# A gated state-space block with a 1.58-bit feed-forward part on one core: the feed-forward steps in another order, and the setup in halves

## The chip, the cores and the metric

The kernel runs on one core of a Trainium2 chip. The metric is the device time of one execution in microseconds (us), lower is better. The kernel before takes 265.46 us (median of 3 runs, 264.85 to 266.59).

## What is computed

`x` is [4 batches, 256 tokens, 256 channels], the context [4, 256, 128]. Cut to what matters:

```python
xc    = causal depthwise conv (4 taps) of in_proj_w @ ctx        # [256, 256] per batch
u     = silu(xc + conv_b)
x_dbl = x_proj_w @ u                 # 40 rows: 8 for delta, 16 B, 16 C
delta = softplus(dt_proj_w @ x_dbl[:8] + dt_proj_b)
state = state * exp(delta * A) + (delta * u) * B   # over 256 tokens, 16 states per channel
y     = (sum over states of state * C + D * u) * silu(layernorm(x))
x     = x + tanh(g_xattn) * y
h     = act_quant(layernorm(x))                    # 8 bit, per token
inter = silu(h @ w_gate.T) * (h @ w_up.T)          # [256, 1024] per batch, ternary weights
x     = x + tanh(g_ffn) * act_quant(hadamard(inter)) @ w_down.T
```

## The kernel before

Everything is written out by hand per engine; each engine runs its list in order, and semaphores tie the lists together. There is no scheduler.

*The scan.* The 16 states of a batch are taken two at a time: 8 steps per batch, 32 in all. Step g needs on ScalarE four exponentials (`decays`, line 823), on GpSimd the input term token by token (`drives`, line 1105), on TensorE its transposes into PSUM (`drive_rows`, 407) and the row of C spread over the partitions (`C_rows`, 447), on VectorE two scans (`scan`, 1230) and one product (`times_C`, 1272), and on TensorE the sum (`accumulate`, 463). In the loops over `k` (batch) and `s` (step, g = 8k + s) VectorE runs `scan(g + 1)` and then `times_C(g)`. The transposes of step g wait for the scan that last read their bank.

*The feed-forward part.* While batch k is scanned, batch f = k - 1 is normalised, quantised to 8 bits and sent through gate and up, and batch p = k - 2 gets its Hadamard transform, quantisation and down product, each in pieces for the two halves of 128 tokens, t = 0 and 1. In order: `residual`, `stats2` (VectorE, 1292 to 1302), `rstd2` (ScalarE, 907), `second_rstd` (1311), `second_norm` (ScalarE), `token_scale` (1326), `scale_tokens` (ScalarE, 923), `round_tokens` (1341), `tokens_T` (TensorE, 557), `gate` (593), `silu_gate` (ScalarE, 929), `up` (593), `gate_times_up` (VectorE, 1352), three folds on GpSimd (`fold_tile`, 1130), `inter_T` (612), `inter_out` (ScalarE, 933), `hadamard_mm` (632), `absmax2` (VectorE, 1360), `quant_down` (ScalarE, 939), `round_down` (1368), `q2_T` (649), `q2_out`, `down` (659), `result` (1380). After the last batch the same pieces run without a scan beside them: the tail.

*The front of a batch.* `in_proj` (492) multiplies the context by four weight copies, one per tap; `silu_u` gives u; `x_dbl` (508) gives rows for B and C and 8 rows for delta, which `dt_rows` copies and `dt_proj` (525) multiplies; `softplus` (889 to 894, ScalarE) with `softplus_tail` (GpSimd) gives delta; `high_pieces` and `split` (1283 to 1285) cut B and C into three bf16 parts; `du_T` turns delta * u. For batch 0 the projection runs without taps (`first_in_proj`, 370), ScalarE and VectorE add the taps (`first_conv`, 1242), and VectorE does the tail of softplus itself (`delta_on_vector`, 1250 to 1254). The PSUM bank X holds the transposes, projections and delta rows of batches 2 and 3 in turn, which is where many waits come from.

*The setup.* SyncE issues the loads in one order: first context, in_proj_w, conv_b, x_proj_w, dt_proj_w, dt_proj_b, D, the other contexts, w_gate, x, w_up, w_down. VectorE takes the three sums |w| (`weight_abs`, 1385), the first before, the second behind the statistics of x (`first_norm`, 1409), the third in step 0.

```python
def silu_gate(f, t):
    act.wait_ge(pe_gate, LC * f + t + 1)
    act.wait_ge(dve_gs, f + 1)
```

## Time and profile before

| | |
|---|---|
| median of 3 runs | 265.46 us (264.85 to 266.59) |
| profiled execution, its own time | 265.58 us |
| its span, first to last instruction | 263.8 us |
| mean granted TensorE clock | 0.883 of full |
| busy: TensorE / VectorE / ScalarE / GpSimd | 187.3 / 213.9 / 157.3 / 147.5 us |
| start of `residual` of batches 0, 1, 2, 3 | 82.65 / 127.54 / 174.37 / 219.89 us |

The span is 1.8 us shorter than the time of the same execution; what lies around it is the same for both kernels. A time in the rows below is counted from the first instruction. The four starts of `residual` cut the span into setup with batch 0, batches 1, 2 and 3, and tail.

### The profile page before, as it was taken

The page shows a single profiled execution, that of the slowest core. Times are in us where ns is not written, and L with a number is a line of the kernel's source. Part 1 is how long each engine was busy: PE and PEld are TensorE (multiplying, and loading weights), DVE is VectorE, ACT ScalarE, POOL GpSimd, SP SyncE. Part 2 cuts the span into 40 slices and gives each one's busy share as a digit, 9 for nine tenths or more (in the row PEclk, how much of TensorE's full clock was granted, in tenths as well). Part 3 has the DMA queues.
Part 4 walks back from the last instruction along what each step waited for, and adds up shares of the span by engine and source line. Part 5 has one row for each costly group of instructions (what it writes and reads, how often), then busy time and mean ns, then how long its engine had stood idle before and what let it go on. Part 6 is the DMA issues. An engine that isn't in the chain of part 4 may idle for free. (4 is left out here: it accounts for less than half of the span.)

```text
span 263.8 us, 3694 instructions
## 1 busy us (share of the span) xinstructions
PE 187.3 (71%) x1209; PEld 155.8 (59%) x1216; DVE 213.9 (81%) x340; ACT 157.3 (60%) x271; POOL 147.5 (56%) x213
## 2 busy tenths in 40 slices
PE   3779489895595569867667787675596768474945
PEld 2547388794494468647557666564485547342944
DVE  4489997898989499579989897998959775579872
ACT  1685996949234556994776799735748504650040
POOL 1100890999961096039999942999930399008500
PEclk9999855899779559999997999999979988989597
DMA  3891000000000000000000000000000000000001
GB/s 60 268 363 75 1 4 0 0 1 2 0 0 2 0 0 1 2 1 0 0 2 0 0 20 4 20 4 0 0 0 24 0 20 2 0 0 1 20 22 40
DMA packets 8149, 6.34 MB, mean 24 GB/s; under 512 B 2202, under 2 KB 7874, under 8 KB 8130
## 3 DMA queue, kind: packets, MB, share of 16 engines
q1 hardware_dynamic: 7154, 6.02, 7.1%
q10 hardware_dynamic: 976, 0.09, 0.3%
q8 instruction: 10, 0.16, 0.3%
q14 instruction: 9, 0.07, 0.1%
HBM read 5.05 MB, written 1.05 MB: 23 GB/s over the span
## 5 line engine op out<-in xcount | busy, mean ns | idle before, releaser
L1105 POOL TENSOR_SCALAR driveT<-duT,BT 128x256 f32<-128x256 f32 x120 | 62.2, 538 | 41.0 <-issue 21.3
L823 ACT ACTIVATE decay<-delta,zero_c,aneg 128x255 f32<-128x255 f32 x128 | 65.2, 589 | 1.7 <-DVE delta L1254 1.6
L1230 DVE TENSOR_TENSOR_SCAN state<-decay,BC 128x512 f32<-128x512 f32 x30 | 36.4, 1213 | 4.4 <-issue 4.3
L1272 DVE TENSOR_TENSOR prod<-state,BC 128x1024 f32<-128x1024 f32 x32 | 38.5, 1204 | 0.6 <-issue 0.6
L463 PE MATMUL PY<-id,prod 128*128 128x128 f32 x256 | 37.9, 297 | 1.4 <-DVE x L1294 1.0
L1230 DVE TENSOR_TENSOR_SCAN state<-decay,UP 128x512 f32<-128x512 f32 x30 | 35.8, 1193 | 0.0
L463 PEld LDWEIGHTS PY<-id,prod 128*128 128x128 f32 x256 | 32.8, 154 | 2.5 <-issue 1.2
L447 PE MATMUL BC<-bc,sel 96*128 96x256 bf16 x64 | 13.1, 288 | 27.4 <-DVE prod L1272 27.3
L1130 POOL TENSOR_TENSOR wnat<-wnat 128x512 f32<-128x512 f32 x18 | 22.9, 1274 | 15.9 <-DVE wnat L1352 15.2
L933 ACT COPY hT<-GP 128x1024 f32<-128x1024 f32 x8 | 8.1, 1010 | 35.0 <-PE GP L612 35.0
L407 PE MATMUL BC<-id,driveT 128*128 128x128 f32 x120 | 21.2, 305 | 10.9 <-POOL driveT L1105 10.8
L407 PEld LDWEIGHTS BC<-id,driveT 128*128 128x128 f32 x120 | 16.0, 161 | 14.6 <-POOL driveT L1105 12.8
L447 PEld LDWEIGHTS BC<-bc,sel 96*128 96x128 bf16 x64 | 5.2, 101 | 32.7 <-issue 31.6
L1131 POOL TENSOR_TENSOR wnat<-wnat 128x512 f32<-128x512 f32 x18 | 22.9, 1275 | 0.0
L407 PE MATMUL UP<-id,driveT 128*128 128x128 f32 x120 | 20.0, 293 | 0.8 <-DVE state L1230 0.8
L407 PEld LDWEIGHTS UP<-id,driveT 128*128 128x128 f32 x120 | 15.6, 153 | 1.5 <-issue 1.5
L593 PE MATMUL GP<-wT,qT 128*128 128x512 bf16 x49 | 13.0, 381 | 3.5 <-ACT wq L929 2.7
L1352 DVE SCALAR_TENSOR_TENSOR wnat<-GP,us,wq 128x1024 f32<-128x1024 f32 x7 | 9.0, 1284 | 7.2 <-issue 5.6
L612 PE MATMUL GP<-id,wnat 128*128 128x128 f32 x64 | 9.9, 306 | 5.1 <-POOL wnat L301 3.2
L300 POOL TENSOR_TENSOR wnat<-wnat 128x160 f32<-128x160 f32 x6 | 4.1, 684 | 14.9 <-DVE wnat L1352 14.6
L280 POOL TENSOR_SCALAR spa<-spe 128x512 f32<-128x512 f32 x3 | 1.9, 619 | 18.4 <-ACT spl L894 18.4
L612 PEld LDWEIGHTS GP<-id,wnat 128*128 128x128 f32 x64 | 8.4, 160 | 5.8 <-DVE wnat L301 3.5
(208 smaller groups left out, 412.7 us busy)
## 6 DMA issues: line engine op xcount, KB each, us to landing
wnat<-in_L_ffn_w_gate_dram SPq DMA_DIRECT2D x1, 1024.0 KB, 9.6
xs<-in_x_dram SPq DMA_DIRECT2D x1, 1024.0 KB, 12.0
wnat<-in_L_ffn_w_up_dram SPq DMA_DIRECT2D x1, 1024.0 KB, 11.5
wnat<-in_L_ffn_w_down_dram SPq DMA_DIRECT2D x1, 1024.0 KB, 11.3
out_dram<-ot SPq DMA_DIRECT2D x8, 128.0 KB, 1.7
ctxs<-in_ctx_dram SPq DMA_DIRECT2D x1, 384.0 KB, 7.1
ctxs<-in_ctx_dram SPq DMA_DIRECT2D x1, 128.0 KB, 2.8
inw<-n_L_xattn_in_proj_w_dram SPq DMA_DIRECT2D x1, 128.0 KB, 2.6
```

The costliest lines, as they stand in the source:

```text
L407: last = nc.tensor.transpose(drive_bank(h)[:, L * n + P * c:L * n + P * (c + 1)], driveT[:, m % RING, c, n, P * h:P * (h + 1)], id32[:])
L447: last = nc.tensor.matmul(PC[:, L * n:L * (n + 1)], row_pick(DS + NB * j + n), bc3[:, b, :], start=True, stop=True)
L463: last = nc.tensor.matmul(PY[:, E * c + P * h:E * c + P * (h + 1)], prod[:, g % RING, h, n, P * c:P * (c + 1)], id32[:], is_transpose=True ...
L593: last = nc.tensor.matmul(ffn_bank(f, t)[:, 512 * i:512 * (i + 1)], qT[:, h, P * t:P * (t + 1)], w[:, h, 512 * i:512 * (i + 1)], start=(h ...
L612: last = nc.tensor.transpose(GP[:, P * a:P * (a + 1)], fold[:, t, P * a:P * (a + 1)], id32[:])
L823: last = nc.scalar.activation(decay[:, m % RING, h, n, 1:L], delta[:, b % 2, h, 1:L], ACT.Exp, bias=zero_c[:], scale=aneg[:, h, NB * j + n ...
L1105: last = nc.gpsimd.tensor_scalar(driveT[:, m % RING, c, n], duT[:, b % 2, c], BT[:, b % 2, c, NB * j + n:NB * j + n + 1], 1.0, ALU.mult, A ...
L1130: nc.gpsimd.tensor_tensor(dst[:, :, 0, :], src[:, :, 0, :], src[:, :, 1, :], ALU.add)
L1131: nc.gpsimd.tensor_tensor(dst[:, :, 1, :], src[:, :, 0, :], src[:, :, 1, :], ALU.subtract).then_inc(done, 1)
L1230: nc.vector.tensor_tensor_scan(state[:, g % STATES, h].rearrange("p n l -> p (n l)"), decay[:, g % RING, h].rearrange("p n l -> p (n l)"), ...
L1272: nc.vector.tensor_tensor(prod[:, g % RING].rearrange("p h n l -> p h (n l)"), state[:, g % STATES].rearrange("p h n l -> p h (n l)"), PC. ...
L1352: nc.vector.scalar_tensor_tensor(out=inter[:, t], in0=ffn_bank(f, t)[:], scalar=us[:, t:t + 1], in1=sg[:, t], op0=ALU.mult, op1=ALU.mult). ...
```

## The change

*Setup.* delta comes from u by one product: `delta_weights` multiplies x_proj_w's first 8 rows by dt_proj_w once (into `dtuT`, 256 x 256), and `delta_raw(n)` is four calls of u by that matrix instead of `dt_rows` and `dt_proj`'s two calls on 8 rows; `x_dbl` has 96 columns instead of 104. The first projection, the first convolution, the first u, the first driving terms and the exponentials signal by halves of the 256 channels. On TensorE the transposes of dt_proj_w, which wait for x_proj_w too, stand ahead of `first_in_proj`. x is loaded ahead of the other contexts and w_gate, dt_proj_w on ScalarE's queue. `first_norm` stands ahead of the first delta and ahead of all three sums |w|, which follow behind the first drives, in step 0 and in step 1. The copies `inwT` and `ctxT` on ScalarE stand behind the first delta and behind decays(0) and decays(1); `in_proj(1)` needs both.

*Steps.* The diff of the loops, cut to the places spoken of (`up(f, 0)` follows `gate(f, 0)`; `hadamard_mm(f, 0)` and `absmax2(p, 0)` are earlier; GpSimd runs five steps ahead):

```diff
+LEAD = 5
             def up(f, t):
-                if f == B - 1:
-                    pe.wait_ge(act_sg, LC * f + t + 1)
-                elif t == 0:
-                    pe.wait_ge(act_sg, LC * f + 2)
-                else:
-                    pe.wait_ge(dve_mul, LC * f + 1)
+                pe.wait_ge(act_sg, LC * f + t + 1)
...
             setup()
+            delta_weights_T()
             first_in_proj()
-            setup_weights()
+            delta_weights()
+            setup_rows()
...
                     if s == 3:
-                        if k == 0:
-                            du_T(1)
+                        if k < B - 1:
+                            du_T(k + 1)
+                        if new:
+                            gate(f, 0)
                         if old:
                             down(p, 0)
-                        if new:
-                            gate(f, 0)
-                        if front:
+                        if k == 0:
                             in_proj(n, 1)
+                        if new:
+                            up(f, 0)
                     if s == 4:
...
+                        if new:
+                            gate(f, 1)
+                            up(f, 1)
...
                     if s == 7:
...
-                            inter_T(f, 0)
+                            hadamard_mm(f, 0)
...
                     if s == 0:
+                        if old:
+                            quant_down(p, 0)
+                        if new:
+                            rstd2(f)
                         if 1 <= k < B - 1:
                             softplus(k + 1)
...
             p, f = B - 2, B - 1
+            absmax2(p, 0)
             residual(f)
```

The first place on TensorE's list, from its start: before,

```order
L343 MATMUL GP<-id,ctxs 128x128 x2
L347 MATMUL GP<-id,inw 128x128 x2
L370 MATMUL GP<-ctxT,xn 128x256 x2
L354 MATMUL PY<-id,xpw 128x40 x2
L358 MATMUL BC<-id,dtw 104x128 x2
L363 MATMUL UP<-id,inwk 128x128 x8
L508 MATMUL GP<-u,xpwT 104x256 x2
L525 MATMUL GP<-dtlo,dtwT 128x256 x2
```

and now (dtw are dt_proj_w's rows, xn holds in_proj_w turned, dtuT the product of the two small weights):

```order
L355 MATMUL GP<-id,ctxs 128x128 x2
L359 MATMUL GP<-id,inw 128x128 x2
L373 MATMUL BC<-id,dtw 8x128 x2
L366 MATMUL GP<-ctxT,xn 128x256
L366 MATMUL X<-ctxT,xn 128x256
L380 MATMUL BC<-dtwT,xpw 128x256
L380 MATMUL UP<-dtwT,xpw 128x256
L386 MATMUL PY<-id,xpw 128x40 x2
L550 MATMUL GP<-u,dtuT 128x256 x2
L550 MATMUL UP<-u,dtuT 128x256 x2
L532 MATMUL GP<-u,xpwT 96x256 x2
```

The dt_proj_w transposes moved ahead of the first projection, the tap copies (L363) went behind the delta product, and delta no longer waits for `x_dbl`.

The second place is VectorE at the turn from batch 1 to batch 2. Before:

```order
L1272 TENSOR_TENSOR prod<-state,BC 128x1024
L1230 SCALAR_TENSOR_TENSOR state<-decay,BC 128x512
L1230 SCALAR_TENSOR_TENSOR state<-decay,UP 128x512
L1272 TENSOR_TENSOR prod<-state,BC 128x1024
L1292 TENSOR_TENSOR PY<-PY,szT 128x512
L1294 TENSOR_TENSOR x<-PY,xs 128x512
```

and now:

```order
L1272 TENSOR_TENSOR prod<-state,BC 128x1024
L1228 SCALAR_TENSOR_TENSOR state<-decay,BC 128x512
L1228 SCALAR_TENSOR_TENSOR state<-decay,UP 128x512
L1360 TENSOR_REDUCE am<-GP 128x1
L1361 TENSOR_SCALAR am<-am 128x1
L1362 RECIPROCAL sc<-am 128x1
L1363 TENSOR_SCALAR dq<-am,wdn 128x1
L1272 TENSOR_TENSOR prod<-state,BC 128x1024
L1292 TENSOR_TENSOR PY<-PY,szT 128x512
L1294 TENSOR_TENSOR x<-PY,xs 128x512
```

`absmax2(p, 0)` now stands behind the second next scan, one step earlier, between the batches' products; it needs the Hadamard product of step 7.

The third place is TensorE at steps 3 and 4 of batch 2 (qT the quantised tokens, q the same before the transpose, driveT the driving terms). Now:

```order
L459 MATMUL X<-id,du 128x128 x4
L616 MATMUL GP<-wT,qT 128x512 x4
L679 MATMUL UP<-wT,q2T 128x256 x8
L616 MATMUL GP<-wT,qT 128x512 x4
L432 MATMUL BC<-id,driveT 128x128 x4
L432 MATMUL UP<-id,driveT 128x128 x4
L472 MATMUL BC<-bc,sel 128x256 x2
L488 MATMUL PY<-id,prod 128x128 x8
L669 MATMUL UP<-id,wq 128x128 x8
L616 MATMUL GP<-wT,qT 128x512 x8
```

The second L616 is `up(f, 0)`, so driveT's transposes and everything behind stand behind the first silu; the last one is `gate(f, 1)` and `up(f, 1)` together. Before, both gates came first, with one step's pieces between them, and each `up` a step later.

## Rows read from the trace of the kernel before

**Rows 1.** The page: busy time of each engine, its share of the span.
```profile
PE 187.3 (71%) x1209; PEld 155.8 (59%) x1216; DVE 213.9 (81%) x340; ACT 157.3 (60%) x271; POOL 147.5 (56%) x213
```

**Rows 2.** Stretches: us, busy us of PE, PEld, DVE, ACT, POOL, PEclk, DMA, GB/s.
```profile
33.07:45.11 12.04, 11.46 (x44) 9.69 (x45) 10.66 (x11) 9.66 (x21) 6.68 (x11) 0.50 0.01 2
45.11:82.65 37.54, 29.04 (x220) 26.27 (x218) 33.79 (x34) 24.00 (x46) 30.80 (x43) 0.86 0.00 1
82.65:127.54 44.89, 32.31 (x203) 26.48 (x205) 36.36 (x53) 29.41 (x55) 22.43 (x31) 0.85 0.00 1
127.54:174.37 46.83, 34.34 (x263) 29.14 (x266) 42.87 (x66) 34.79 (x58) 37.93 (x53) 0.96 0.02 7
174.37:216.54 42.17, 28.74 (x220) 24.01 (x222) 35.88 (x57) 23.11 (x34) 26.79 (x37) 0.95 0.02 7
216.54:219.89 3.35, 3.31 (x18) 3.31 (x19) 0.00 (x1) 0.00 (x0) 3.27 (x3) 0.59 0.02 5
```

**Rows 3.** Timeline, setup, TensorE: start, us, line, tiles [idle before].
```profile
5.32 2.08 PE L370 MATMUL GP<-ctxT,xn 128*128 128x256 f32 x4 [0.52 <-DVE xn L1428]
8.76 0.43 PE L354 MATMUL PY<-id,xpw 40*128 40x40 f32 x2 [1.37 <-DMA dtw<-n_L_xattn_dt_proj_w_dram]
14.36 2.07 PE L525 MATMUL GP<-dtlo,dtwT 8*128 8x256 f32 x4 [0.45 <-ACT dtlo L879]
22.27 3.76 PE L492 MATMUL GP<-ctxT,inwT 128*128 128x256 f32 x8 [0.52 <-ACT ctxT L991]
```

**Rows 4.** Timeline, setup, ScalarE and VectorE.
```profile
7.57 1.02 ACT L965 ACTIVATE conv<-GP,cb,cw 128x256 f32<-128x256 f32 x2 [3.04 <-PE GP L370]
11.08 0.72 ACT L978 ACTIVATE u<-conv,zero_c 128x512 f32<-128x512 f32 x1 [0.57 <-DVE conv L1242]
...
14.29 2.29 DVE L1385 TENSOR_REDUCE wsum<-wnat 128x1 f32<-128x2048 f32 x1 [3.25 <-DMA wnat<-in_L_ffn_w_gate_dram]
23.50 0.69 DVE L1254 TENSOR_TENSOR delta<-spl,spr 128x512 f32<-128x512 f32 x1
39.05 0.40 DVE L1283 TENSOR_TENSOR bc<-GP,high 64x256 bf16<-64x256 f32 x1
```

**Rows 5.** Timeline, batch 0, VectorE: two roundings of the weights.
```profile
57.24 1.26 DVE L1397 TENSOR_SCALAR wq<-wnat 128x2048 bf16<-128x2048 f32 x1
62.73 3.00 DVE L1397 TENSOR_SCALAR wq<-wnat 128x2048 bf16<-128x2048 f32 x1 [0.89 <-POOL wnat L1136]
```

**Rows 6.** Timeline, start of batch 1, VectorE.
```profile
86.34 1.22 DVE L1230 TENSOR_TENSOR_SCAN state<-decay,BC 128x512 f32<-128x512 f32 x1
...
92.19 0.34 DVE L1311 TENSOR_SCALAR ve<-mv,r 128x1 f32<-128x1 f32 x2 [3.52 <-ACT r L908]
```

**Rows 7.** Timeline, batch 2, steps 2 to 5, TensorE, ScalarE, VectorE.
```profile
146.69 2.00 PE L632 MATMUL GP<-had,hT 128*128 128x128 f32 x16
155.31 1.21 ACT L929 ACTIVATE wq<-GP,zero_c,gs 128x1024 f32<-128x1024 f32 x1
157.72 1.21 ACT L929 ACTIVATE wq<-GP,zero_c,gs 128x1024 f32<-128x1024 f32 x1 [0.60 <-PE GP L593]
159.05 1.03 PE L593 MATMUL GP<-wT,qT 128*128 128x512 bf16 x4
160.17 1.28 DVE L1352 SCALAR_TENSOR_TENSOR wnat<-GP,us,wq 128x1024 f32<-128x1024 f32 x1 [1.30 <-issue]
```

**Rows 8.** Timeline, end of batch 3 and tail, TensorE and VectorE.
```profile
216.58 1.97 PE L463 MATMUL PY<-id,prod 128*128 128x128 f32 x8 [0.40 <-DVE prod L1272]
218.34 1.51 PE L472 MATMUL PY<-diag,u 128*128 128x128 f32 x8
...
228.96 3.30 PE L632 MATMUL BC<-had,hT 128*128 128x128 f32 x16
232.74 0.91 PE L593 MATMUL GP<-wT,qT 128*128 128x512 bf16 x3 [0.49 <-DVE qT L1345]
...
228.39 1.22 DVE L1360 TENSOR_REDUCE am<-UP 128x1 f32<-128x1024 f32 x1
```

More of the change, by code:

```diff
@@ L31 @@
 DVE_COLS = 88
-DT0 = 96
+ROWS = 3 * 2 * DS
 class Chain:
@@ L171, in gated_ssm_ffn @@
         bank6, bank7 = UP[:, 0:512], UP[:, 512:1024]
-        mean1, ve1, nt1 = (UP[:, 8 * i:8 * (i + 1)] for i in range(3))
+        first = sb("first", [P, 3, B * LC])
+        mean1, ve1, nt1 = (first[:, i] for i in range(3))
         wgT = wT[:, 0].rearrange("p (h i) -> p h i", h=HALF)
@@ L348, in setup, with first_in_proj, delta_weights_T, delta_weights @@
                 last.then_inc(pe_setup, 1)
-            def setup_weights():
-                pe.wait_ge(ld_small, 16 * 2)
+            def first_in_proj():
+                pe.wait_ge(dve_setup, 2)
+                for h in range(HALF):
+                    nc.tensor.matmul(first_half(h), inw0T[:, P * h:P * (h + 1)], ctxT[:, 0, :],
+                                     start=True, stop=True).then_inc(pe_xin0, 1)
+            def delta_weights_T():
+                pe.wait_ge(ld_small, 16 * 2)
+                for h in range(HALF):
+                    last = nc.tensor.transpose(PC[0:DR, P * h:P * (h + 1)], dtw[:, h], id32[:])
+                last.then_inc(pe_setup, 1)
+            def delta_weights():
+                pe.wait_ge(act_dtw, 1)
+                for h in range(HALF):
+                    nc.tensor.matmul(delta_weight_bank(h), xpw[0:DR, P * h:P * (h + 1)], dtwT[:],
+                                     start=True, stop=True).then_inc(pe_setup, 1)
+            def setup_rows():
                 for h in range(HALF):
@@ L356, in setup_weights, with setup_taps @@
                 last.then_inc(pe_setup, 1)
-                for h in range(HALF):
-                    last = nc.tensor.transpose(PB[0:DT0 + DR, P * h:P * (h + 1)], dtw[:, h], id32[:])
-                last.then_inc(pe_setup, 1)
-                pe.wait_ge(dve_inwk, 2)
-                for k in range(DC):
+            def setup_taps(part):
+                pe.wait_ge(dve_inwk, part + 1)
+                pe.wait_ge(act_spread, 1)
+                for k in range(2 * part, 2 * part + 2):
                     for h in range(HALF):
@@ L364, in setup_weights @@
                 last.then_inc(pe_setup, 1)
-            def first_in_proj():
-                pe.wait_ge(dve_setup, 2)
-                for h in range(HALF):
-                    last = nc.tensor.matmul(bank4[:, L * h:L * (h + 1)], inw0T[:, P * h:P * (h + 1)], ctxT[:, 0, :],
-                                            start=True, stop=True)
-                last.then_inc(pe_xin, 1)
             def setup_late():
                 pe.wait_ge(ld_ctx, 16)
-                pe.wait_ge(act_setup, 1)
+                pe.wait_ge(dve_xpw, 1)
                 for b in range(1, B):
@@ L1018, in _ @@
                             softplus(1)
-                            gate_out(0)
-                        if new:
-                            rstd2(f)
-                        if old:
-                            quant_down(p, 0)
                         if new:
@@ L1081, in _ @@
             second_norm(f)
+            inter_out(p, 1)
             scale_tokens(f)
-            inter_out(p, 1)
-            quant_down(p, 0)
             silu_gate(f, 0)
@@ L1152, in _ @@
             last.then_inc(pool_diag, 1)
-            drives(DVE_DRIVES)
+            for m in range(DVE_DRIVES, LEAD):
+                drives(m)
             norm_z(0)
-            for m in range(DVE_DRIVES + 1, AHEAD):
-                drives(m)
             for k in range(B):
```

376 lines of the change are left out of this document (181 added, 195 removed).

## Prediction, made before the changed kernel was run

> **What bounds the kernel now.** I read the page first: no engine is full; VectorE is the busiest with 213.9 of 263.8 us [rows 1]. Then the stretches between the four starts of `residual` [rows 2]. VectorE's idle time is a stretch's length less its busy time: batch 1 44.89 - 36.36 = 8.5 us, batch 2 46.83 - 42.87 = 4.0 us, batch 3 up to its last product 42.17 - 35.88 = 6.3 us, then 3.35 us with VectorE empty, until TensorE has summed the last state. The scan is a chain through VectorE (no step can begin before its list reaches it), so a microsecond saved there is saved in the span, and one hidden elsewhere is not. Then the timeline at the largest waits: in the setup VectorE waits 3.25 us for w_gate [rows 4]; in batch 1 it waits 3.52 us for the second norm's root, which on ScalarE stands behind a whole softplus [rows 6]; gate times up waits in each batch, 1.30 us in batch 2 [rows 7]. The change touches all three places, so the question is what stands there afterwards. VectorE's work is the same but for one small copy taken over from ScalarE.
>
> The sum is a walk through the new lists with the durations of the rows, stretch by stretch, against the profiled execution (span 263.8, time 265.58, so 1.8 us around it); its time is 0.12 us above the median of the runs, which I neglect.
>
> **Setup and batch 0: -0.6 us.** `first_in_proj` runs at 5.32 now [rows 3]. In the new list the transposes of dt_proj_w stand ahead of it, and they wait for two loads, x_proj_w's too. Today both have landed at 8.76, where TensorE's wait ends [rows 3]; ScalarE's first tap starts at 7.57 [rows 4]. The landing of the two with dt_proj_w on the other queue isn't shown: it lies between 5.32 (no delay) and 8.76 (as today). I take 7.7, nearer to the late end, since x_proj_w stays behind conv_b in its queue. Then 0.7 us of transposes, 1.0 us for half a product (2.08 for two), and the first tap starts at 9.5 instead of 7.57. The halves give back a little, and u(0) ends at 13.5 instead of 11.80 (+1.7). `delta_raw` doubles the calls: `dt_proj` takes 2.07 for two, so four take 4.1, but ScalarE starts on the first half after 2.05. In place of `x_dbl`, a copy and `dt_proj` that makes 17.7 for the end of delta's product. After softplus and VectorE's tail, delta starts its last operation at 22.4 instead of 23.50: -1.1, because the statistics of x (3.4 us) now fill the wait in which VectorE stood for the weights.
>
> That gain is spent at once. The first sum |w| (2.29 us) was in that wait and is now in line. And `in_proj(1)` needs `ctxT`, whose copy stands behind decays(1): TensorE idles from about 27 to 31.3 and then needs 3.76 for the first half of the projection, as at 22.27 [rows 3], and about 1.9 for the second. It ends at 37.3, u(1), `x_dbl(1)` and the cast of its rows follow, and VectorE's `split(1)`, at 39.05 today [rows 4], starts at 40.7 after a wait of 3.3 us. Scan 3 starts at 47.5 instead of 45.11: +2.4. From there to `residual(0)` the same work follows. VectorE's idle time there is 37.54 - 33.79 = 3.8 us, of which some 2 go (the weights' sum is long ready, drives are five ahead), and a rounding that took 3.00 against 1.26 for the same tile [rows 5] falls behind GpSimd's scaling: -1. Together -0.6; bounds -2.5 (loads at 5.32) and +2.5 (loads at 8.76, nothing of the idle time gained).
>
> On that rounding: the 3.00 us one starts with GpSimd scaling the next weights. The Trainium skill says (SBUF — State Buffer, section "SBUF: two separate sides") that VectorE and GpSimd share one pair of SBUF ports, held for a whole instruction by whoever started first. By that rule slow roundings come back wherever they meet a GpSimd pass, and the last 1 us would not be gained; the sum would be 1 us higher. On the loads it says (DMA: Bandwidth & Descriptors, section "Issuing engines are not separate DMA queues") that the queues of two engines run on the same DMA engines and that a second queue saves only issue time. By that rule the two loads land at 8.76 as before, and the setup costs 1.0 us more; no row here shows these loads on different queues.
>
> **Batch 1: +0.9 us.** The 8.5 us of waits go. `rstd2` stands ahead of softplus, so the 3.52 us vanish. What is late next: `second_norm` still stands behind softplus(2), which waits for `delta_raw(2)`. TensorE's clock is low there, and two calls of `dt_proj` took 2.07 at the low clock [rows 3], so four take about 4: x's norm comes 1.1 us after VectorE is ready for it. The scaled tokens come 1.0 late. `up(0, 0)` stands right behind `gate(0, 0)` and waits for the silu, which on ScalarE stands behind the tokens' copy, an exponential group, a copy of duT and a table load; VectorE waits 3.2 us for the first gate times up and 0.6 for the second. Sum of new waits 5.9. Then the early `absmax2(0, 0)` falls into this stretch: 1.7 us of work (an absmax of this form is 1.22, [rows 8], its three small ones the rest) and a wait: after the last product of batch 1 TensorE needs the rows of C, the sum (0.9 at full clock), D * u (0.9) and the Hadamard product (2.00, [rows 7]), 4.05 together, against 2.25 for two scans (1.22 each, overlapping a little, [rows 6]): 1.8. 44.9 - 8.5 + 5.9 + 3.5 = 45.8.
>
> **Batch 2: +2.5 us.** 4.0 of idle go. One absmax goes out and one comes in, with 1.8 of wait. The tokens and the Hadamard of half 1 are 0.7 late. `quant_down(0, 1)` ends 1.5 after VectorE wants to round it: it stands behind the tokens' copy, which waits for TensorE's transposes behind the scan. Gate times up: today both gates' silus (155.31 and 157.72) come before `up` at 159.05 and VectorE waits 1.30 [rows 7]. Now `up(1, 0)` follows the first silu at once, about 2.5 us sooner, but VectorE wants it 2.25 + 1.1 sooner, and copy_duT is ahead: 1.8. The second gate now waits for the first gate times up, then comes its silu behind a copy of q2, then `up`: 6.0 us from `up` to `up` against 4.6 of work: 1.1 (the rest overlaps). New waits 6.9, less 0.4 of slow small operations: 46.8 - 4.0 + 6.9 - 0.4 = 49.3.
>
> **Batch 3 to its last product: -4.2 us.** 6.3 of idle go, absmax2(1, 0) is already done (1.7), the new waits are 1.5 + 1.2 + 1.1 + 0.6 and some small ones, 4.6, less 0.8 of slow roundings: 42.2 - 6.3 - 1.7 + 4.6 - 0.8 = 38.0.
>
> **Tail: +2.2 us.** VectorE stands empty for 3.35 us [rows 2] while TensorE does the last sum (1.97) and D * u (1.51) [rows 8]. The new list has `inter_T` ahead of that sum and the Hadamard product behind it, and `absmax2(2, 0)` stands ahead of `residual(3)`. At TensorE's full clock that is 0.9 + 0.9 + 0.9 + 2.0 and absmax2 1.7, 5.9 us until `residual(3)`; at half clock, as the 0.59 of that stretch says of today [rows 2], up to 8.3. I take 6.8: +3.4. In return absmax2 (228.39) and its rounding leave the chain between the tokens and their transpose. But today the Hadamard of half 1 (3.30) covers them, and the gate at 232.74 starts right behind it [rows 8]. Now that product is ahead of the tokens' transpose and bound by `inter_out` on ScalarE: gain 1.2. Bounds 0 and +4.4.
>
> Sum: -0.6 + 0.9 + 2.5 - 4.2 + 2.2 = +0.8, so 265.58 + 0.8 = 266.4; I say 266.5.
>
> **Rivals.** (1) The walk counts every handover in full, and the new waits are half of what it says: TensorE keeps the full clock through batches and tail and the two loads land early. Then tail 0 instead of +2.2, setup -2.5 instead of -0.6: 266.4 - 2.2 - 1.9 = 262.3. For it: the clock is 0.96 and 0.95 in batches 2 and 3 [rows 2], and `inter_T` fills a gap. Against it: 0.59 at the end, and first_in_proj's wait is in the list. (2) Slower: the Hadamard product at each turn runs at the low clock. It took 3.30 and not 2.00 in the tail [rows 7, 8]; the turn then costs 1.3 more in batches 1 and 2, and the tail takes its bound (+2.2): 266.4 + 4.8 = 271.2. It decides from about 0.85 granted at the turns. The Trainium skill (TensorE: Matmul & The Clock Gate, section "What's actually happening") says that the throttled clock is the default and activity releases it; the trace agrees, 0.50 after TensorE's pause before 33.07 [rows 2]. By that rule the longer pauses before each `up` speak for this rival. (3) The change doesn't do what it says: x lands no earlier, first_norm runs behind 17 us as today, and the first delta comes 2 us later: 268.4.
>
> **How the numbers follow.** My forecast 0.45, rival 1 0.25, rival 2 0.23, rival 3 0.07. About 1% is what a measurement of this kernel can tell from no change: 262.8 and 268.1 are the bounds. Of my forecast's 0.45 (264.0 to 269.0) 0.38 lie within, 0.02 below and 0.05 above; rival 1 gives 0.21 faster, 0.04 same; rival 2 is all slower; rival 3 half slower. Faster 0.23, same 0.45, slower 0.32. The range reaches to both rivals: 261.0 to 271.5.
>
> **What would show it.** Right: the gap ahead of L1311 is gone in batch 1; VectorE waits some 1.8 us ahead of absmax2 at both turns and 4 or more in the tail; the first tap starts after 9 us; split(1) waits about 3 us. Wrong: absmax2 without a wait, the first tap before 8 us, or batch 2 shorter than 46.8 us.

## The result and the profile after

The changed kernel takes 273.42 us (median of 4 runs, 272.92 to 276.38) where the kernel before, run beside it on the same chip, takes 266.02: a ratio of 1.029, 95% interval 1.020 to 1.039. It is slower by 7.4 us. The prediction was 266.5 us with a range up to 271.5. It had the sign right (+0.8 us) and missed the size: a time within 1% of the kernel before was held likeliest, and the measured one lies outside the range.

The profiled execution of after is its longest, 276.38 us with a span of 274.6; the other three have spans of 271.1 to 271.8. Executions of one kernel differ here, so the places come from the profiles and the sizes from the medians. Ratios and their intervals leave out executions more than 1.5% above a kernel's fastest and medians don't, so the two can differ, most for abs0_behind_stats, whose ratio rests on two of its twelve executions.

The page of after, busy time by engine, against [rows 1]:

```profile
PE 190.8 (70%) x1232; PEld 157.9 (58%) x1236; DVE 215.2 (78%) x341; ACT 155.5 (57%) x268; POOL 146.9 (53%) x212
```

VectorE has 1.3 us more work in a span 10.8 us longer: this is waiting. The stretches, cut as in [rows 2] (the first from scan 3, the next from `residual` to `residual`; columns as there):

```profile
45.83:83.98 38.15, 28.05 (x206) 24.55 (x206) 34.86 (x35) 22.13 (x42) 29.30 (x41) 0.87 0.00 1
83.98:129.26 45.28, 34.21 (x239) 28.42 (x240) 38.50 (x58) 33.00 (x60) 32.58 (x43) 0.96 0.01 1
129.26:180.51 51.25, 37.22 (x267) 31.41 (x268) 42.12 (x66) 34.64 (x59) 38.58 (x55) 0.90 0.02 6
180.51:222.84 42.33, 29.91 (x191) 25.00 (x193) 33.47 (x53) 18.69 (x29) 17.90 (x24) 0.79 0.02 7
222.84:230.18 7.34, 5.66 (x40) 5.47 (x38) 1.58 (x6) 1.01 (x1) 4.03 (x4) 0.82 0.00 0
```

Length less VectorE's busy time is its idle time: 9.1 us in batch 2 and 8.9 in batch 3, against 4.0 and 6.3 before. All the waits of VectorE over a microsecond between `residual(1)` and `residual(3)` (timeline; the bracket holds the idle time ahead and what ended it, `issue` where the profile shows nothing that did):

```profile
145.61 0.45 DVE L1341 TENSOR_SCALAR q<-xn 128x512 bf16<-128x512 f32 x1 [1.69 <-ACT xn L940]
153.49 0.70 DVE L1368 TENSOR_SCALAR wq<-ctxs 128x1024 bf16<-128x1024 f32 x1 [2.26 <-ACT ctxs L956]
159.58 1.28 DVE L1352 SCALAR_TENSOR_TENSOR wnat<-GP,us,wq 128x1024 f32<-128x1024 f32 x1 [1.65 <-issue]
165.24 1.28 DVE L1352 SCALAR_TENSOR_TENSOR wnat<-GP,us,wq 128x1024 f32<-128x1024 f32 x1 [1.03 <-issue]
177.74 1.22 DVE L1360 TENSOR_REDUCE am<-GP 128x1 f32<-128x1024 f32 x1 [1.88 <-PE GP L652]
195.44 0.43 DVE L1341 TENSOR_SCALAR q<-xn 128x512 bf16<-128x512 f32 x1 [1.92 <-ACT xn L940]
197.36 1.23 DVE L1360 TENSOR_REDUCE am<-GP 128x1 f32<-128x1024 f32 x1 [1.49 <-PE GP L652]
204.69 0.69 DVE L1368 TENSOR_SCALAR wq<-ctxs 128x1024 bf16<-128x1024 f32 x1 [2.27 <-ACT ctxs L956]
210.32 1.28 DVE L1352 SCALAR_TENSOR_TENSOR wnat<-GP,us,wq 128x1024 f32<-128x1024 f32 x1 [1.19 <-issue]
215.98 1.28 DVE L1352 SCALAR_TENSOR_TENSOR wnat<-GP,us,wq 128x1024 f32<-128x1024 f32 x1 [1.03 <-issue]
228.54 1.22 DVE L1360 TENSOR_REDUCE am<-GP 128x1 f32<-128x1024 f32 x1 [5.69 <-PE GP L652]
```

The new waits have names: the rounding of half 1 (L1368, twice), the absmax at the turn (177.74; the turn of batch 1 has the same 1.88 at 126.49) and in the tail (228.54), and q (L1341). The four gate-times-up operations (L1352) each start 1.1 us after TensorE has begun the `up` that they need, at 158.45, 164.11, 209.19 and 214.85. In the tail, the first gate product starts 20.1 us after the last product (242.92), and 16.2 us in before (232.74 in [rows 8] less 216.54 in [rows 2]).

The setup (timeline; ScalarE's rows, then VectorE's, against [rows 3, 4]):

```profile
6.59 0.56 ACT L984 ACTIVATE conv<-GP,cb,cw 128x256 f32<-128x256 f32 x1 [0.98 <-PE GP L366]
10.79 0.29 ACT L987 ACTIVATE tg<-gates,zero_c 128x2 f32<-128x2 f32 x1 [2.99 <-DMA alog<-in_L_xattn_A_log_dram]
11.91 0.51 ACT L992 ACTIVATE u<-conv,zero_c 128x256 f32<-128x256 f32 x1
...
13.83 2.71 DVE L1409 BATCH_NORM_STATS2 st<-xs 128x6 f32<-128x256 f32 x8 [3.44 <-DMA xs<-in_x_dram]
17.94 0.43 DVE L1248 TENSOR_SCALAR spa<-spe 128x512 f32<-128x512 f32 x1 [0.44 <-ACT spe L908]
21.18 0.69 DVE L1254 TENSOR_TENSOR delta<-spl,spr 128x512 f32<-128x512 f32 x1
38.90 0.42 DVE L1283 TENSOR_TENSOR bc<-GP,high 64x256 bf16<-64x256 f32 x1 [1.09 <-ACT high L893]
```

delta comes 2.3 us earlier than before (21.18 against 23.50), but `split(1)` at 38.90 against 39.05 keeps 0.15 of that, and `residual(0)` starts 1.3 us late.

### The profile page after: what moved, and what is told of

It is laid out like the page before. It is cut to its first block and busy times, and to the rows that moved or that the text cites. A ratio compares the mean times of both kernels' runs of the same rounds, so it can differ in the third digit from the quotient of the medians.

```text
span 274.6 us, 3736 instructions
## 1 busy us (share of the span) xinstructions
PE 190.8 (70%) x1232; PEld 157.9 (58%) x1236; DVE 215.2 (78%) x341; ACT 155.5 (57%) x268; POOL 146.9 (53%) x212
## 5 line engine op out<-in xcount | busy, mean ns | idle before, releaser
L488 PE MATMUL PY<-id,prod 128*128 128x128 f32 x256 | 40.8, 312 | 2.9 <-DVE x L1294 2.9
L488 PEld LDWEIGHTS PY<-id,prod 128*128 128x128 f32 x256 | 35.7, 164 | 4.2 <-issue 3.6
L432 PE MATMUL BC<-id,driveT 128*128 128x128 f32 x120 | 19.2, 285 | 10.7 <-DVE state L1228 9.2
L432 PEld LDWEIGHTS BC<-id,driveT 128*128 128x128 f32 x120 | 14.8, 150 | 14.3 <-issue 10.8
L616 PE MATMUL GP<-wT,qT 128*128 128x512 bf16 x52 | 13.6, 380 | 13.1 <-ACT wq L946 10.6
L432 PEld LDWEIGHTS UP<-id,driveT 128*128 128x128 f32 x120 | 14.7, 150 | 5.6 <-issue 4.9
L1352 DVE SCALAR_TENSOR_TENSOR wnat<-GP,us,wq 128x1024 f32<-128x1024 f32 x7 | 9.0, 1284 | 10.6 <-issue 10.6
L616 PEld LDWEIGHTS GP<-wT,qT 128*128 128x128 bf16 x56 | 4.7, 98 | 19.5 <-ACT wq L946 13.6
L635 PE MATMUL GP<-id,wnat 128*128 128x128 f32 x64 | 10.9, 326 | 6.2 <-POOL wnat L315 3.2
L1360 DVE TENSOR_REDUCE am<-GP 128x1 f32<-128x1024 f32 x5 | 6.1, 1225 | 11.0 <-PE GP L652 10.9
```

Source lines behind the costliest of these rows:

```text
L432: last = nc.tensor.transpose(drive_bank(h)[:, L * n + P * c:L * n + P * (c + 1)], driveT[:, m % RING, c, n, P * h:P * (h + 1)], id32[:])
L488: last = nc.tensor.matmul(PY[:, E * c + P * h:E * c + P * (h + 1)], prod[:, g % RING, h, n, P * c:P * (c + 1)], id32[:], is_transpose=True ...
L616: last = nc.tensor.matmul(ffn_bank(f, t)[:, 512 * i:512 * (i + 1)], qT[:, h, P * t:P * (t + 1)], w[:, h, 512 * i:512 * (i + 1)], start=(h ...
L635: last = nc.tensor.transpose(GP[:, P * a:P * (a + 1)], fold[:, t, P * a:P * (a + 1)], id32[:])
```

## Experiments

Thirteen runs of twelve kernels, on several chips, each beside the kernel before on one chip. "Against before" is the difference of these two medians; the median of before itself lies between 265.23 and 266.65 us from chip to chip.

| kernel | median us | against before | ratio, 95% interval |
|---|---|---|---|
| after | 273.42 | +7.4 | 1.029 (1.020 to 1.039) |
| setup_alone | 268.62 | +3.4 | 1.010 (1.005 to 1.014) |
| abs1_back | 272.14 | +6.9 | 1.022 (1.015 to 1.029) |
| tail_only | 271.80 | +5.2 | 1.019 (1.014 to 1.024) |
| abs0_behind_stats | 267.87 | +2.6 | 0.994 (0.986 to 1.001) |
| all_three | 263.69 | -3.0 | no interval |
| all_three_again | 263.31 | -2.3 | 0.982 (0.974 to 0.990) |
| before_rstd_first | 264.05 | -1.2 | 0.994 (0.990 to 0.999) |
| setup_rstd_first | 267.48 | +0.8 | 1.004 (1.000 to 1.008) |
| delta_twice | 270.77 | +4.7 | 1.016 (1.010 to 1.023) |
| rows_in_loop | 263.23 | -2.4 | 0.990 (0.987 to 0.994) |
| norm_first | 264.05 | -2.0 | 0.992 (0.988 to 0.997) |
| norm_scale_first | 266.04 | 0.0 | 0.995 (0.990 to 1.000) |
| before_norm_first | 265.13 | -1.0 | 0.997 (0.993 to 1.002) |

**setup_alone: one part of the change alone.** The new setup, delta from u and scans by halves, with the four engines' loops in the order of before. Against before, in TensorE's loop:

```diff
                     if s == 0:
                         if k == 0:
-                            dt_proj(1)
+                            delta_raw(1)
                             gate_T(0)
                         if 1 <= k < B - 1:
-                            dt_proj(k + 1)
+                            delta_raw(k + 1)
```

> The changed setup, delta from u by one product, and the scans that start by halves, with the loops of the four engines in the order of the kernel before. Theory A (the new order of the feed-forward part makes the loss, by waits that it puts on VectorE): the setup and batch 0 cost 1.3 us more than before (83.98 against 82.65 us to the first residual), the rest is as before, so 267.3 us (265.5 to 269). Theory B (the setup leaves the whole program with a lower granted clock, 0.842 against 0.883, and the loss comes with it): 271 us or more, and batches 2 and 3 longer than before's 46.8 and 42.2 us even in the old order.

268.6 us, 3.4 over before: above theory A's value but in its range, below theory B's. Its batch 2 is 48.3 us long, 1.5 longer than before's, and its batch 3 is 40.6, 1.6 shorter, so B's two longer batches aren't there, nor is B's lower clock (0.890 in its profile, 0.883 in before's). The new setup with delta from u has a cost of its own, and by these medians a somewhat larger part of the loss, 4.0 us, is the order's. In batch 1 the wait that the full change removes is longer than in [rows 6]:

```profile
94.98 0.33 DVE L1332 TENSOR_SCALAR ve<-mv,r 128x1 f32<-128x1 f32 x2 [5.05 <-ACT r L936]
```

**abs1_back: one row of the order undone.**

```diff
                     if s == 3:
                         if new:
                             round_tokens(f)
-                        if old:
-                            absmax2(p, 1)
...
                         scan(g + 1, 0)
                         scan(g + 1, 1)
...
                     if s == 3:
                         if k == 0:
                             weight_means()
+                        if old:
+                            absmax2(p, 1)
```

> After, with the absolute maximum of the second half (absmax2(p, 1)) moved back behind the scans of slot 3. Theory A: ahead of the scans it holds them by 1.9 us with its wait and 1.7 with its work; TensorE's drive rows of that slot wait for the scans, the transposes of q stand behind the drive rows, ScalarE's copy of qT behind those, and its scaling for round_down(p, 1) behind that; so the waits of 2.26 and 2.27 us ahead of round_down(p, 1) and of 1.49 ahead of absmax2(1, 1) all go: 4 to 6 us off 273.4, 268.5 us (267 to 270.5). Theory B (TensorE at 1.2 GHz is what is late, whatever stands ahead): the wait ahead of round_down(p, 1) shrinks by less than half and others grow, 272.5 to 274.

The waits went as theory A says: none ahead of the rounding L1368 and of absmax2(1, 1) is left over 0.5 us in batches 2 and 3. This shows the chain of theory A, with one number put right: the 1.9 us is q's wait (195.44 above), and absmax2's own is 1.49 in batch 3 and nearly nothing in batch 2 (146.15, right behind q). Batches 2 and 3 are 50.1 and 40.6 us long, 1.1 and 1.7 shorter than after's. But batch 1, in which the edit changes nothing, took 48.1 us here and 45.3 in after, so stretches of one list differ by more than that between two executions. The median fell only by 1.3 us (0.5 against before), and the intervals of the two ratios overlap. It lies between the two theories' ranges, nearer to B's. Alone the edit is worth little; see all_three.

**abs0_behind_stats and tail_only: two microseconds of work put into a wait.**

```diff
-                        if old:
-                            absmax2(p, 0)
                     times_C(g)
                     if s == 0:
                         if new:
                             residual(f)
                             stats2(f, dve_ln_link.begin(dve, f))
+                        if old:
+                            absmax2(p, 0)
```

and the same in the tail, with `rstd2` ahead of `quant_down(p, 0)` on ScalarE in both places. tail_only has the edit in the tail alone.

> After, with absmax2(p, 0) behind residual and stats2 at both turns and in the tail, and ScalarE's rstd2 ahead of its quant_down(p, 0). Theory A: residual and stats2 (2.4 us at 129.26 to 131.7) cover the wait of 1.88 us at both turns and 2.6 of the 5.69 us in the tail: 6.4 us less, of which about 1.2 comes back where round_down(p, 0) of batch 3 has no split ahead of it; 268.2 us (266.5 to 270). Rival (the Hadamard product of the tail is the end of another chain, so that residual comes earlier but the first gate product doesn't): the turns' 3.8 us alone, 269.6, or with the turns' gain lost in q's wait too, 272 to 273.

> After, with absmax2(p, 0) behind residual and stats2 in the tail alone (and rstd2 ahead of quant_down(p, 0) there); the turns stay. In abs0_behind_stats the first gate product came 17.6 us after the last product, against 20.1 in after and 16.2 in before. If the tail's order is worth that alone, 2.5 us go: 270.9 us (269.5 to 272), and the other 3 of the 5.5 us that abs0_behind_stats gained are the turns' (1.88 us, twice). Rival: the tail holds all 5.5 us and the turns' waits come back elsewhere, 268 us.

267.9 us as theory A had it, and 271.8 for the tail alone, inside its range. By the medians against before, the tail's part is 2.2 us (7.4 to 5.2) and the turns' 2.6 (5.2 to 2.6), not the 3.8 of two waits: 1.2 us stand ahead of `round_down` in batch 3, as expected. That the two together are a gain is clear (ratios of 1.029 and 0.994, with intervals apart), but how it splits isn't: the ratios 1.029, 1.019 and 0.994 give the turns the larger part, while in the profiles the tail alone is 5.5 us shorter (46.24 us in tail_only, 46.16 in abs0_behind_stats, 51.76 in after, from the last product to the end). What is left in abs0_behind_stats:

```profile
151.85 0.69 DVE L1368 TENSOR_SCALAR wq<-ctxs 128x1024 bf16<-128x1024 f32 x1 [1.65 <-ACT ctxs L956]
165.26 1.28 DVE L1352 SCALAR_TENSOR_TENSOR wnat<-GP,us,wq 128x1024 f32<-128x1024 f32 x1 [2.69 <-issue]
182.17 2.00 DVE L1368 TENSOR_SCALAR wq<-ctxs 128x1024 bf16<-128x1024 f32 x1 [1.16 <-ACT ctxs L956]
225.09 0.70 DVE L1292 TENSOR_TENSOR PY<-PY,szT 128x512 f32<-128x512 f32 x1 [3.74 <-PE PY L497]
```

**all_three: both, and the tanh of the gates behind u(0).**

```diff
-            act.wait_ge(ld_gate, 16 * 3)
-            nc.scalar.activation(tg[:], gates[:], ACT.Tanh, bias=zero_c[:]).then_inc(act_gate, 1)
             for h in range(HALF):
                 ...
             last.then_inc(act_u, 1)
+            act.wait_ge(ld_gate, 16 * 3)
+            nc.scalar.activation(tg[:], gates[:], ACT.Tanh, bias=zero_c[:]).then_inc(act_gate, 1)
```

> After with absmax2(p, 0) behind stats2 (turns and tail), absmax2(p, 1) behind the scans, and the tanh of the gates with its wait for the last load behind u(0). By the runs so far: 267.9, less 1.3 to 2.8 for absmax2(p, 1) (its medians and the two batches of its profile), less at most 0.4 for the tanh, since VectorE is at the first norm, for which x lands at 13.8, until 17.5 and waited 0.44 us for softplus behind it, however early u(0) is: 265.5 us (263.5 to 267), level with before. Rival (each wait removed is taken up by the next in line, q's and the gate products'): 267 to 268.5, no gain over abs0_behind_stats. Second rival (the early u(0) starts the whole chain of the setup earlier): first residual at 81 us and not at 83, 263 us.

> The same kernel as all_three, beside rows_in_loop on one chip, for an interval against before: 263.7 us by the first call, so a ratio of 0.985 to 0.995 if that holds.

263.7 and 263.3 us: 10 us faster than after, under the expected 265.5, and faster than before, by 1.8% by the ratio of the second run (just past the expected 0.985) and 0.9% by its medians. In all_three's profile u(0) began its second half at 10.36 instead of after's 11.91, and delta came 0.55 us earlier relative to x's landing (20.26 with x at 13.45, against 20.79 with x at 13.43 in abs0_behind_stats). So the tanh was worth half a microsecond to delta; at `residual(0)` (82.84 and 81.85 in the two profiles, 82.27 in abs0_behind_stats) no gain can be told. The stretches of batches 1 to 3, in all_three_again and in abs0_behind_stats:

```profile
81.85:125.88 44.03, 34.55 (x227) 27.98 (x228) 36.93 (x53) 30.41 (x57) 29.54 (x40) 0.92 0.01 1
125.88:173.10 47.22, 36.27 (x271) 30.13 (x270) 42.07 (x66) 35.76 (x61) 37.55 (x53) 0.93 0.02 7
173.10:214.51 41.41, 28.23 (x206) 23.91 (x205) 34.93 (x57) 20.47 (x31) 22.16 (x29) 0.85 0.02 7
```

```profile
82.27:126.30 44.03, 34.30 (x226) 27.94 (x228) 36.94 (x53) 30.40 (x57) 29.54 (x40) 0.92 0.01 1
126.30:176.91 50.61, 36.21 (x270) 30.95 (x270) 42.22 (x65) 35.62 (x61) 39.64 (x56) 0.93 0.02 6
176.91:221.34 44.43, 27.76 (x205) 23.27 (x205) 36.06 (x57) 20.46 (x31) 19.65 (x27) 0.86 0.02 7
```

Batch 1 is the same to 0.01 us, at the same granted clock. Batches 2 and 3, the only ones in which absmax2(p, 1) stands, are 3.4 and 3.0 us shorter at nearly the same clock. So in this pair its place is worth 6.4 us, and in abs1_back's profile only 2.8. The direction agrees in the medians against before (4.9 to 5.6 us here with the tanh, 0.5 in abs1_back) and in the ratios (1.2% here, 0.7% there, with overlapping intervals), the size doesn't: batch 2 took 51.25 us in after and 53.84 in tail_only, whose lists are the same up to the tail. That the gains aren't additive is therefore likely but not shown. A reading that fits: in abs1_back the chain of absmax2(p, 0) at the turn still stood (its 1.88 us are in that profile at both turns); with that gone too, the chain of half 1 was the one that held both batches.

**before_rstd_first and before_norm_first: what of the change is good for the old kernel.** The first moves one call on ScalarE:

```diff
                     if s == 1:
...
-                        if new:
-                            rstd2(f)
...
                     if s == 0:
+                        if new:
+                            rstd2(f)
                         if 1 <= k < B - 1:
                             softplus(k + 1)
```

The second moves `softplus(k + 1)` behind `second_norm(f)` of slot 1 as well.

> The kernel before with one line moved on ScalarE: rstd2(f) ahead of softplus(k + 1) in slot 0. Theory A (the wait of 3.52 us ahead of L1311 in batch 1 is the one clear gain of the new order): 2.5 to 3.5 us faster than before, 263 us. Rival (the next wait, for scaled tokens or for the gate product, is late by the same chain and takes it): 265.5 to 266.5, and the waits behind it in batch 1 grow by what goes.

> before_rstd_first with second_norm(f) ahead of softplus(k + 1) too. Its norms weren't waited for (no wait ahead of amax in the loop), but the scaled tokens were, 1.33 and 1.23 us in batches 2 and 3, and the first gate product 2.54, 2.04 and 1.37. If the norm's place matters only where the longer product from u stands ahead of softplus: no gain, 264 us (263 to 265). If the chain norm, scale, q, gate starts earlier here too: 262 us.

The wait of 3.52 us of [rows 6] is gone and 1.2 us of the median with it, between theory and rival: part of it was taken up later, as in batch 2, where the first gate times up now waits 2.04 us (1.30 in [rows 7]). The norm's place adds nothing (1.0 us under before where the first had 1.2): softplus then stands between norm and scaling, and the wait is ahead of q (1.78 us in batch 1, where there was none).

**setup_rstd_first, delta_twice and rows_in_loop: the setup or the product from u?** The first is setup_alone with `rstd2` ahead of softplus. The second repeats the product:

```diff
                 for h in range(HALF):
-                    for i in range(HALF):
-                        last = nc.tensor.matmul(delta_half(n, h), dtuT[:, i, P * h:P * (h + 1)],
+                    for _ in range(2 if n > 0 else 1):
+                        for i in range(HALF):
+                            last = nc.tensor.matmul(delta_half(n, h), dtuT[:, i, P * h:P * (h + 1)],
                     ...
                     last.then_inc(pe_draw, 1)
```

The third takes it out of batches 1 to 3 of all_three, with rows of x_dbl copied by ScalarE and a second, shifted copy of dt_proj_w:

```diff
+                if n >= 1:
+                    pe.wait_ge(act_dtlo, n)
+                    for h in range(HALF):
+                        nc.tensor.matmul(delta_half(n, h), dtwT2[DT0:ROWS, P * h:P * (h + 1)], dtlo[DT0:ROWS, :],
+                                         start=True, stop=True).then_inc(pe_draw, 1)
+                    return
```

> setup_alone with rstd2 ahead of softplus. In setup_alone L1311's counterpart waited 5.05 us in batch 1, where before waited 3.52, since the eight products that make delta from u end later than the two of dt_proj did. Theory D (the product from u costs only by what stands behind softplus on ScalarE): the whole wait goes, and the time is that of before_rstd_first, 264.05, plus what the setup costs to the first residual, 0.9: 265 us (263.5 to 266.2). Theory E (the setup and the longer product cost by themselves, in TensorE's time and in the clock of what follows): the distance of 3.4 us between setup_alone and before stays, 267.4 us (266.3 to 269).

> setup_rstd_first with the eight products that make delta from u computed twice in slot 0 of batches 0 to 2 (the same operands into the same bank, the second product replaces the first; nothing else changes). One product group took 1.89 us on TensorE where the clock was granted at 2.4 GHz and 3.57 to 3.75 at 1.2. Theory F (the product from u is what setup_rstd_first pays over before_rstd_first, 3.4 us by their medians, 2 by their ratios to before, by way of softplus, the second norm and the waits for scaled tokens behind it): as much again per batch, 2 to 4 us over 267.5, so 270.5 us (269.5 to 272), with new waits of some 2 us ahead of amax in batches 1 and 2. Theory G (the product is covered; the setup itself holds the loss): 267.5 to 268.5.

> all_three with delta of batches 1 to 3 made as in the kernel before, from dt rows of x_dbl by two products of 8 rows (and ScalarE's dt_rows copy, 0.36 us, ahead of copy_BT); batch 0 keeps the product from u. delta_twice paid 3.3 us by the medians for computing the longer product once more in three batches. Theory F (the product from u costs 1 us or more a batch, in TensorE's time ahead of softplus): 263.7 less 2 to 3.5, 261 us (259.5 to 262.5), and below all_three_again of the same call. Theory G (with rstd2 ahead of softplus the product's place is covered, and what delta_twice paid was only the second one): level with all_three_again within 1 us.

By its time setup_rstd_first came out as theory E says. But the kernel before took 266.65 us on that chip and 265.23 on the one that the theories were worked out from, and against before, 0.8 us, it lies between the two (D -0.2, E 2.2). Of the 3.4 us, 2.6 went with the one call, but the same call gives before 1.2 us, so 2.0 stay between the two kernels. delta_twice spoke for the product as their cause (3.3 us for three repetitions, or 3.9 against before), though the waits came elsewhere than expected: ahead of amax there was 1.33 us in batch 1 (0.93 in setup_rstd_first) and none over 0.75 in batch 2, and ahead of absmax2(0, 0) 3.25 (1.52). rows_in_loop spoke against it: 263.2 us beside 263.3, as theory G says, and batches 1 to 3 of the two profiles, both with a granted clock of 0.864, agree to 0.4 us. (By the ratios, 0.990 and 0.982, it would even be the slower one.) In it the product in batch 1 was indeed short, and softplus began 5.6 us after `residual` instead of 7.6 in all_three. Part of what it gained there was lost on TensorE: its in_proj of batch 1 took 3.23 us, that of all_three 1.88, the duration at 2.4 GHz. TensorE's two products in rows_in_loop, then in all_three:

```profile
85.59 1.77 PE L557 MATMUL X<-dtlo,dtwT 8*128 8x256 f32 x4 [1.14 <-issue]
93.39 3.23 PE L522 MATMUL X<-ctxT,inwT 128*128 128x256 f32 x8
```

```profile
86.61 3.75 PE L550 MATMUL X<-u,dtuT 128*128 128x256 f32 x8 [0.27 <-issue]
93.01 1.88 PE L516 MATMUL X<-ctxT,inwT 128*128 128x256 f32 x8
```

So in the order of all_three the product from u costs nothing that can be measured. In the old order this wasn't tried: delta_twice shows that a second product costs there, not what the first one does. What makes the 2.0 us is therefore open. The setup can be a part of it: `residual(0)` starts at 83.1 us on the mean of the seven profiles that have the new setup with the tanh in its place, and at 82.2 on that of the three with the old setup. But the seven lie between 81.9 and 84.0, so even these 0.9 us aren't clear of the spread.

**norm_first and norm_scale_first: attempts at more.** On all_three, ScalarE's softplus behind the norm; norm_scale_first has `inter_out(p, 1)` behind `scale_tokens(f)` as well.

```diff
                     if s == 1:
...
                         if new:
                             second_norm(f)
+                        if 1 <= k < B - 1:
+                            softplus(k + 1)
...
                     if s == 0:
...
-                        if 1 <= k < B - 1:
-                            softplus(k + 1)
```

> all_three with ScalarE's second_norm ahead of softplus(k + 1) in batches 1 and 2. In all_three's batch 1 rn and mr were there at 90.2 us, softplus ran from 90.46 to 93.45 and the norm behind it; VectorE waited 0.93 us for the norm and 0.78 for the scaled tokens, and 4.16 for the first gate product. With the norm first these 1.7 us go in batch 1 and most of the 0.9 in batch 2, and the gate product's wait doesn't grow, since its chain (norm, scale, q, gate) starts 3 us earlier: 263.7 less 2 to 3, 261.3 us (260 to 263). Rival (softplus, now later, holds POOL's tail, the next batch's delta or the decays of slot 1): level or slower, 264 to 266.

> norm_first with inter_out(p, 1) behind scale_tokens(f) on ScalarE. The waits of 1.72 and 1.92 us ahead of q in batches 2 and 3 of all_three were for a scaling that stood behind the 1.0 us copy to hT (and gate_out); with the copy behind it about 1 us goes in each: 260 us (258.5 to 262). Rival (the Hadamard product of the second half and the C rows behind it on TensorE come later by as much, and VectorE's products wait for them): no gain over norm_first.

Both missed, and came out as their rivals had it: 264.1 and 266.0 us, no gain over all_three. In norm_first the waits of 0.93 and 0.78 us of batch 1 became one of 1.79 ahead of q, since softplus now sits between norm and scaling. In norm_scale_first the wait ahead of q fell as intended, from 2.56 to 1.65 us in batch 2 and from 1.93 to 1.04 in batch 3, and the copy's lateness came back at once, at absmax2(0, 1) (1.53) and in both batches at the rounding behind it (1.07).

## Why the prediction was wrong

Differences are of the profiled executions, 10.8 us in all where 0.8 were forecast; by the medians it is 7.4, as the profiled execution of after is some 3 us longer than the other three. Of a single stretch the size is known to 2 or 3 us only: batch 1 took 45.28 us in after and 47.65 and 48.13 in tail_only and abs1_back, where its lists are the same.

- **Setup and batch 0: -0.6 forecast, +1.3 measured.** The step "I take 7.7" for the landing of the two loads failed: the transposes of dt_proj_w ran at 4.52, and the first tap at 6.59, which I had named as a sign against me.

  TensorE's wait at 8.76 of [rows 3] counts both loads, and I had held x_proj_w to be the one that stays late. In after x_proj_w, whose place is unchanged, had landed by 4.5, and so had dt_proj_w, now issued at 1.7 us on ScalarE instead of 2.7 behind four others. It is no accident of one execution: the transposes ran at 4.5 to 5.6 in all twelve profiles with the new setup, and the wait for the two loads ended at 7.4 to 8.8 in the three with the old one, each time at dt_proj_w by the profile. When x_proj_w landed there isn't shown; conv_b, ahead of both and unmoved, took 5.7, 5.4 and 3.4 us to land in the three and 2.4 to 3.0 in the twelve, so the move also sped up a load that it didn't touch. By the Trainium skill (DMA: Bandwidth & Descriptors, "Issuing engines are not separate DMA queues") a second queue would have saved its issue time alone; here 1.0 us of earlier issue went with over 4 us of earlier landing, and the measurement decides. Whether the other queue did it or the place in the list, third instead of fifth, wasn't separated.

  The early tap was then wasted, as the tanh, which I had not looked at, waited 2.99 us for A_log's load (8.9 us in before by its issue and its time to landing, 10.8 in after). Up to scan 3 the stretch was still better than forecast (+0.7 against +2.4). What failed was the -3 behind it: that part took 38.15 us against 37.54 in [rows 2]. VectorE's idle time there fell by 0.5 us, not 2, with a new wait of 2.79 for weight transposes. Its busy time rose by 1.1 instead of falling by 1, since the slow roundings moved and stayed (7.1 us for the three, 5.8 in before):

```profile
57.02 3.02 DVE L1397 TENSOR_SCALAR wq<-wnat 128x2048 bf16<-128x2048 f32 x1 [0.32 <-POOL wnat L1140]
63.31 1.46 DVE L1397 TENSOR_SCALAR wq<-wnat 128x2048 bf16<-128x2048 f32 x1
69.24 2.58 DVE L1397 TENSOR_SCALAR wq<-wnat 128x2048 bf16<-128x2048 f32 x1
...
81.41 0.69 DVE L1401 TENSOR_SCALAR wT<-UP 128x1024 bf16<-128x1024 bf16 x1 [2.79 <-PE UP L705]
```

  The first one lies in GpSimd's scaling of three weights in a row, 55.02 to 61.87. That is the rule of the Trainium skill (SBUF — State Buffer, "SBUF: two separate sides") which the forecast had set aside, and the trace agrees for this one: 3.02 us against 1.26 in [rows 5]. It doesn't agree for every pass of GpSimd: those 1.26 us, from 57.24, began inside GpSimd's normalising of x (L1116, 56.86 to 58.92) and weren't held up.
- **Batch 1: +0.9 forecast, +0.4 measured.** Right in most of its steps: no wait ahead of L1311, 3.31 for the first gate times up (3.2 said), 0.53 for the second (0.6), 1.88 ahead of absmax2 (1.8). The norm wasn't waited for (1.1 said), the scaled tokens 0.64 (1.0 said). That the total fits is partly luck of this execution: its granted clock was 0.96 there, and in tail_only and abs1_back (0.93 and 0.89) the same batch is 2.8 and 3.2 us over before's, with 4.16 and 4.15 ahead of the first gate times up.
- **Batch 2: +2.5 forecast, +4.4 measured.** Right in kind, mis-sized in two terms: the tokens' wait was 1.69 (0.7 said, with the Hadamard product) and the rounding's 2.26 (1.5). The five waits make 8.5 us, and all of VectorE's idle time 9.1, not 6.9.
- **Batch 3: -4.2 forecast, +0.2 measured. This is the step that failed most.** The term that failed is "the new waits are 1.5 + 1.2 + 1.1 + 0.6 and some small ones, 4.6". VectorE's idle time there is 8.9 us, 4.3 more; its busy time fell by 2.4, as forecast (1.7 + 0.8). The term had at most 0.6 for q (1.92) and absmax2(1, 1) (1.49) together, and 1.5 for the rounding (2.27); the two gate times up (1.19 and 1.03) it had. It also took all 6.3 us of idle time as gone, of which 2.77 was the same absmax2(1, 1) in before, a wait that the forecast doesn't name:

```profile
196.19 1.22 DVE L1360 TENSOR_REDUCE am<-GP 128x1 f32<-128x1024 f32 x1 [2.77 <-PE GP L632]
```

  The walk through batch 3 was a copy of the one through batch 2 with its terms cut, though the lists are the same. The mechanism I had half seen ("stands behind the tokens' copy, which waits for TensorE's transposes behind the scan") is at work here: the early absmax2(p, 1) holds the scans, these hold the drive rows, these the tokens' transpose and all behind it. abs1_back shows the chain: with absmax2(p, 1) behind the scans the waits ahead of absmax2(1, 1) and of the rounding went. I priced it as 1.5 us ahead of the rounding in each batch; its place was worth 3.4 and 3.0 us a batch in the pair of profiles under all_three.
- **Tail: +2.2 forecast, +4.5 measured.** `residual(3)` came 7.34 us after the last product (6.8 said, 5.69 us of wait), the first part is right. (The terms named for it, 0.9 + 0.9 + 0.9 + 2.0 + 1.7, make 6.4 and not 5.9, so the low end was set too low.) The gain of 1.2 behind it didn't come: the first gate product starts 12.7 us after `residual(3)`, 12.9 in before, and from `residual(3)` to the end it is 0.5 us longer (44.4 against 43.9). In tail_only the first gate product starts 17.4 us after the last product instead of 20.1, and what follows, the same list, takes 28.9 us at a granted clock of 0.94 instead of 31.7 at 0.76. By the medians 2.2 us of the loss lie in this order of absmax2 and residual.

Of the rivals the slower one, 271.2, came nearest, and not for its reason: the tail took its bound in size (4.5), but the Hadamard product at the low clock isn't in the trace, it took 1.95 us at both turns and ahead of absmax2(2, 0) in the tail, and the turns' waits were 1.88. The upper end of 271.5 was too tight since I took the terms' errors as of either sign; outside batch 1 they all had the same, and in batches 2 and 3 they are handovers that the walk left out or priced too low.

## What to carry to other kernels

Before pulling an operation ahead in an engine's list, see what it will wait for and who is served behind it: an early operation that waits 1.9 us ahead of a scan costs not its wait but the turn of every engine that the scan feeds. Put the work that is ready (here residual and its statistics, 2.4 us) ahead of the operation that isn't; that exchange, absmax2(p, 1) behind the scans and the tanh behind u(0) together took 10 us off the changed kernel. And walk every period of a loop by itself, to the end, with the same list of handovers, also where one of them looks like a copy of the last.

## What the runs showed of the hardware

- The same list takes different times at different granted clocks, although TensorE is idle for three tenths of the time: the tail took 46.34 us at 0.87 in all_three's profile and 48.99 at 0.78 in all_three_again's, the same kernel. Between kernels the mean clock says nothing: rows_in_loop has most of its spans at 260.4 to 261.5 us with 0.863, norm_first, in eight of its twelve executions, 260.2 to 263.5 with 0.883 to 0.902.
- More work may keep the clock. delta_twice was granted over 0.9 in four of its six executions (0.869 to 0.917), setup_rstd_first, the same kernel with each of these products once, in one of twelve, on another chip. rows_in_loop, with the short product, was granted 0.833 to 0.875, and all_three_again beside it on one chip 0.864 to 0.895. A saving on TensorE may be given back in this way, as the 3.23 us of in_proj above against 1.88 are; that it is the cause wasn't tested by itself.
- A rounding that began during GpSimd's scaling of the weights (54.99 to 60.86) took 6.93 us in setup_rstd_first, 3 us past the end of that scaling, and two later roundings of the same form took 1.25 and 1.21 beside GpSimd's driving terms:

```profile
57.01 6.93 DVE L1418 TENSOR_SCALAR wq<-wnat 128x2048 bf16<-128x2048 f32 x1 [1.71 <-POOL wnat L1158]
67.21 1.25 DVE L1418 TENSOR_SCALAR wq<-wnat 128x2048 bf16<-128x2048 f32 x1
```

- The four small operations of the first norm's root took 0.17 us each in before, with the statistics in PSUM, and 0.35 to 0.42 in after, with them in SBUF; GpSimd was at its driving terms in both (27.68 to 31.41 and 25.72 to 34.64). Whether the operands' place or something else makes the difference wasn't tried.

```profile
28.81 0.42 DVE L1216 SCALAR_TENSOR_TENSOR r<-first,r 128x8 f32<-128x8 f32 x1
```
